# The order of VectorE's work within a slot of a cross-attention kernel: sums and reciprocal ahead of outputs, remainders and the subtraction of maxima

## The reference, cut to what matters

```python
# x: (128, 128, 320); ctx: (128, 128, 512); 20 heads of 16 channels
SEGS = [(0, 77), (77, 81), (81, 85), (85, 128)]
q = heads(x @ to_q_w)
out = 0
for (a, e), wk, wv in zip(SEGS, key_weights, value_weights):    # 512 x 320 each
    k, v = heads(ctx[:, a:e] @ wk), heads(ctx[:, a:e] @ wv)
    p = softmax(q @ k.T / sqrt(16))                             # over this segment alone
    out += p @ v
return merge(out) @ to_out_w + to_out_b + x
```

## Time and profile before

| | |
|---|---|
| median of 3 runs | 1812.3 us (1810.25 to 1822.74) |
| the profiled execution's own time | 1827.61 us |
| its span, first to last instruction | 1825.8 us |
| mean granted PE clock | 0.979 |
| busy: PE, PE weight loads, DVE, ACT, POOL | 93%, 76%, 82%, 57%, 68% |
| instructions | 48271 |

### The profile page before, as it was taken

The page is one execution under the profiler, slowest core; times in us unless marked ns, Lnnn a source line. Parts: engine busy times, 40 slices in busy tenths (PEclk is TensorE's granted clock), DMA queues, the critical chain, the costliest instruction groups (busy, mean ns, idle before and its releaser), DMA issues.

```text
span 1825.8 us, 48271 instructions
## 1 busy us (share of the span) xinstructions
PE 1690.6 (93%) x15120; PEld 1383.0 (76%) x15120; DVE 1495.5 (82%) x3536; ACT 1040.9 (57%) x1860; POOL 1249.3 (68%) x1452
## 2 busy tenths in 40 slices
PE   6859999999999999999999999999999999999987
PEld 3547777788777778777777877777787777787765
DVE  4148988988888888888898888889888888888897
ACT  1135666665565566565666656566665655665564
POOL 3237677767766766777776777677677767767644
PEclk9979999999999999999999999999999999999999
DMA  7678987887888787888788788878878887877861
GB/s 281 171 201 194 222 199 208 214 205 211 206 212 198 204 208 198 200 213 205 211 216 201 210 205 219 209 203 215 208 205 200 210 201 202 209 197 180 211 125 37
DMA packets 409172, 366.24 MB, mean 201 GB/s; under 512 B 17137, under 2 KB 380210, under 8 KB 404786
## 3 DMA queue, kind: packets, MB, share of 16 engines
q1 hardware_dynamic: 409138, 365.79, 79.5%
HBM read 216.30 MB, written 149.42 MB: 200 GB/s over the span
## 4 chain that ended last, share of the span: by engine, by line
PE 67%; DVE 17%; issue 8%; ACT 4%; DMA 1%; DVEq 0%; SPq 0%; ACTq 0%; POOL 0%; POOLq 0%
PE job_ps L786 28%; PE ring_ps L852 10%; PE ring_ps L872 8%; PE ring_ps L865 7%; DVE l_seg L667 6%; PE s_ps L825 4%; PE job_ps L802 4%; DVE probs L640 4%; DVE rest L657 2%; DVE m_seg L624 2%; PE ring_ps L753 2%; ACT probs L543 2%; PE job_ps L796 1%; PE job_ps L805 1%; ACT parts L525 1%
## 5 line engine op out<-in xcount | busy, mean ns | idle before, releaser
L463 POOL TENSOR_TENSOR probs<-probs,rl 128x616 f32<-128x616 f32 (+1 forms) x640 | 628.8, 1005 | 362.6 <-DVE rl L678 357.6
L786 PE MATMUL job_ps<-c_in,w_kv 128*128 128x172 f32 (+1 forms) x2560 | 576.9, 368 | 22.0 <-DVE rest L657 22.0
L552 ACT ACTIVATE pT<-ring_ps 128x512 f32<-128x512 f32 x640 | 378.3, 598 | 356.8 <-PE ring_ps L852 348.2
L786 PEld LDWEIGHTS job_ps<-c_in,w_kv 128*128 128x128 f32 x2560 | 424.5, 190 | 111.2 <-DVE rest L657 29.7
L667 DVE TENSOR_REDUCE l_seg<-probs 128x8 f32<-128x616 f32 (+1 forms) x640 | 385.8, 645 | 56.3 <-ACT probs L543 56.3
L852 PE MATMUL ring_ps<-ident,probs 128*128 128x128 f32 x2560 | 389.4, 277 | 9.3 <-DVE y L687 8.0
L640 DVE TENSOR_TENSOR probs<-s_ps,m_seg 128x616 f32<-128x616 f32 (+1 forms) x640 | 387.3, 647 | 0.0
L624 DVE TENSOR_REDUCE m_seg<-s_ps 128x8 f32<-128x616 f32 (+1 forms) x640 | 368.9, 618 | 0.0
L543 ACT ACTIVATE probs<-probs 128x1024 f32<-128x1024 f32 x320 | 337.5, 1055 | 15.8 <-DVE probs L644 15.8
L852 PEld LDWEIGHTS ring_ps<-ident,probs 128*128 128x128 f32 x2560 | 290.4, 143 | 64.5 <-issue 25.4
L657 DVE TENSOR_TENSOR rest<-job_ps,parts 128x512 f32<-128x512 f32 (+1 forms) x192 | 130.7, 681 | 144.6 <-ACT parts L525 144.6
(11 more groups left out here) (47 smaller groups left out, 1402.9 us busy)
## 6 DMA issues: line engine op xcount, KB each, us to landing
q_all<-q_scratch SPq DMA_DIRECT2D x64, 960.0 KB, 8.5
k_all<-k_scratch SPq DMA_DIRECT2D x64, 960.0 KB, 12.7
c_in<-in_cT SPq DMA_DIRECT2D x32, 1024.0 KB, 5.0
x_raw<-in_xT SPq DMA_DIRECT2D x32, 768.0 KB, 4.4
q_scratch<-parts SPq DMA_DIRECT2D x64, 384.0 KB, 3.0
k_scratch<-parts SPq DMA_DIRECT2D x64, 384.0 KB, 2.5
x_res<-in_x SPq DMA_DIRECT2D x128, 160.0 KB, 3.4
out<-y SPq DMA_DIRECT2D x128, 160.0 KB, 2.9
```

Of the source, the lines that this page charges most:

```text
L463: pool.tensor_tensor(pr[:, :, a:e], pr[:, :, a:e], r[:, :, s:s + 1].broadcast_to((P, OH, e - a)), ALU.mult)
L552: act.activation(pT[:, h:h + QH, :], ring_ps[i][:, :].rearrange("p (h s) -> p h s", h=QH), ACT.Copy)\
L786: last = pe.matmul(dst[:, :, a:e], w_kv[:, l, k, i * P:(i + 1) * P], c_in[:, k, :, a:e], start=(k == 0), stop=(k == CK - 1))
```

## The change

In a slot DVE now takes the maxima of octet n+1, then at once the sums and the reciprocal of octet n, then the outputs, the remainders of both kinds, and last the subtraction of the maxima of octet n+1. Before, the order was: maxima of n+1, outputs, remainders of jobs that ended at 0, subtraction of maxima of n+1, sums of n, remainders of jobs that ended at 1, reciprocal of n. All instructions stay as they are, and the other engines are not touched.

```diff
                 if live(gg, G):
                     reduce_max(gg, o)
+                if live(g, G):
+                    sum_up(g, n)
+                    invert(g, n)
                 for at, (nn, kind, what) in enumerate(FILLS):
                     if nn == (n - 1) % NO and kind == "y" and live(g * NB + what, B):
                         add_residual(g + what // NB, what % NB, at % 2)
-                for turn, job in ended(g, n - 1, 0):
-                    if job in SPLITS:
-                        subtract_part(turn, job)
+                for at in range(2):
+                    for turn, job in ended(g, n - 1, at):
+                        if job in SPLITS:
+                            subtract_part(turn, job)
                 if live(gg, G):
                     shift(gg, o)
-                if live(g, G):
-                    sum_up(g, n)
-                for turn, job in ended(g, n - 1, 1):
-                    if job in SPLITS:
-                        subtract_part(turn, job)
-                if live(g, G):
-                    invert(g, n)
```

## The result

| | before | after |
|---|---|---|
| median of the runs | 1816.97 us (1810.25 to 1822.74, 4 runs) | 2037.52 us (2035.76 to 2038.18, 4 runs) |
| profiled execution | 1827.61 us | 2036.92 us |
| mean granted PE clock | 0.979 | 0.950 |

What follows compares the result with a forecast made beforehand. PE was taken to set the pace, waiting on DVE's releases. 1808.7 us without clock falls, plus 145.5 for gates in 30 groups and 5 for the last groups, made 1959; with 71 for the clock, 2030 us, range 1945 to 2085.

Steps and rivals of the forecast that it cites:

- slot 2: The first transposes wait for the output of slot 1's projection: PE 0.73 us later in each group.
- slots 3 and 4: The late subtraction for octet 4 delays slot 4's sums, output and q0's remainder: q1's products start 2.75 us later.
- slot 5: q2's products wait for q1's remainder, which moves ahead of the subtraction of maxima: the 1.72 us wait goes.
- slot 8: kv1's first half waits for kv0's remainder, now behind exponential, sums and reciprocal: PE 3.09 us later.
- The chain through ACT: Each moved release gets PE, ACT copies, exponential, sums and reciprocal in front of it; gates sum to 4.85 us a group.
- The clock: Behind PE's waits in slots 8 and 4, 45 of 60 bring falls to 1.2 GHz, 1.58 us each: 71 us.
- The ends: In the last two groups, two output gates each, 1 to 1.5 us apiece: 5 us added.
- (a): Rival: PE's gates come as worked out in all groups but the clock stays up: 1959 us, chance 0.2.
- (b): Rival: the exponential is exposed in every slot, 10 us a group more than before: 2112 us, chance 0.1.
- (c): Rival: slot 8 costs 3.1 us but slots 2 to 4 nothing, 1.4 us a group: 1855 us, chance 0.05.
- (d): Rival: not slower; second-kind remainders precede the subtraction, q2's 1.72 us wait and its clock falls go: 1757 us, chance 0.04.
- The other two signs: Prediction wrong if slot 8's exponential starts before kv0's copy, or if the period stays under 55 us.

Runs made afterwards that it cites:

- the kernel with the filled wait: The changed kernel with 32 unused transposes on PE in slot 8, just before kv1's products wait for kv0's remainder: 1969.7 us.
- q1's alone: The kernel before, with q1's remainder in slot 5 taken right behind the maxima instead of behind the sums: 1792.8 us, 0.982 of the kernel before.
- q1's and q2's: The kernel before, with q1's remainder (slot 5) and q2's (slot 6) taken right behind the maxima: 1749.8 us, 0.9646 of the kernel before.

## Why the prediction was right

**What bounds it.** PE sets the pace and DVE matters by when it releases PE: shown. With kv0's release alone put back, the other waits stayed the same to 0.01 us.

**The gates.** The no-fall period was put at 57.9 us; it is 57.66 (the kernel with the filled wait). Its starts, to be held against 881.26, 889.92, 896.97 and 910.78:

```profile
1004.45 0.66 PE L849 MATMUL ring_ps<-ident,probs 128*128 128x128 f32 x4 [0.73 <-DVE y L687]
...
1015.80 0.50 PE L799 MATMUL job_ps<-x_hi,w_q 128*128 128x512 f32 x1
...
1020.91 0.49 PE L799 MATMUL job_ps<-x_hi,w_q 128*128 128x512 f32 x1
...
1037.77 2.34 PE L783 MATMUL job_ps<-c_in,w_kv 128*128 128x308 f32 x8 [0.23 <-DVE rest L657]
```

Term by term, from start to start: slot 2 at +0.73, measured +0.81 (24.34 from kv1's start at 980.11, against 23.53 from the one at 857.73, a period of 53.05 ahead of 910.78); slots 3 and 4 at +2.75, measured +2.69 (11.35 against 8.66); slot 5 at -1.72, measured -1.94 (5.11 against 7.05); slot 8 at +3.09, measured +3.05 (16.86 against 13.81). So the worst sized was slot 5: I took the idle time that the row of q2's products shows, and their start gained 0.2 us more than that. The sum is 57.66 - 53.05 = 4.61 us and not 4.85, 138 us in 30 groups and not 145.5.

**The chain through ACT.** Shown twice: the exponential 1.0 us earlier took 1.0 us off the wait, and outputs or remainders in front of the sums took the slot 8 and slot 2 waits away.

**The clock.** The step was 45 falls of 1.58 us, 71 us. The mean period is 60.35 us, so the clock costs 60.35 - 57.66 = 2.69 us a group, 81 us. In the 30 groups the falls are 30 at slot 8 and 21 behind slot 4, 51 rather than 45, at 1.6 us each. The count was a guess between bounds, and its closeness is partly luck: the experiments show that the same wait of 2.17 us brings a fall in 21 of 30 groups (changed kernel), in 10 (filled wait) or in one (kv0's remainder back). The Trainium skill ("TensorE: Matmul & The Clock Gate", "HAM oscillation") tells of a matmul kernel whose wait for data in each round is long enough that PE starts every round at the lower clock. In the changed kernel slot 8's wait of 3.72 us did so in every group, slot 4's of 2.17 us in two groups of three.

**The ends.** 2036.9 - 1808.7 - 138 - 81 = 9 us, against 5. Some 1.6 us of it stand in group 0: the first kv1 products of slot 8 start 4.6 us later than before (164.74 against 160.10), and 3.04 of that is the gate. There PE waits 1.35, 1.34 and 0.34 us for the subtraction, a place at which I had counted nothing. The rest, some 7 us, stands behind the last of the 30 gates of slot 8. How it divides there between waits and clock was not worked out.

**The rivals.** (a), the clock stays up, falls by the window at 0.50. (b), exposure in every slot, had DVE's idle time right and its price wrong: DVE waits 392.9 us for exponentials where it waited 56.3, 11 us a group more, but this is idle time of an engine that has it to spare. The period without falls is 57.66 us and not 63. (c) falls with the waits of 0.73 and 2.17 us in slots 2 and 4. (d) falls for the whole change, but its useful part was real: without the rest it gives 3.5%.

**The signs.** Of the three signs of being wrong, one was set wrongly. It asked whether kv0's remainder starts less than 2 us after the exponential's end. It starts 1.67 us after (1309.52 to 1311.19), so by the sign the chain would be refuted. But the prediction's own working had 1.66 there (911.46 to 913.12), and the experiments show the chain. The other two signs did not come.

## What to carry to other kernels

When an engine's order is changed, don't add up its work; list what it releases (a bank, a buffer) and, for each release, the chain that now stands ahead of it, and compare that with when the waiting engine wants it. An operation that waits for a long chain belongs behind the short releases that others need, even if, as here, this engine is idle a quarter of the time. A release may be moved ahead of work by itself, and the gate behind it has to be looked at in the same step: q1's alone gave 1.8%, q1's and q2's 3.5%.

## What the runs showed of the hardware that was not expected

A short wait of PE may cost again through the clock, and its length alone doesn't say how often: 2.17 us of wait in slot 4 brought PE to 1.2 GHz in 21, 10 or 1 of 30 groups of three kernels, whose other waits and periods differ. What decides it was not shown. Nor is the price of a fall fixed: 1.1 to 2.6 us with the remainders in front of the sums, 1.2 to 1.6 with the filled wait. That is why moving one remainder was worth 171 us where its wait was worth 91. And PE given 3.66 us of useless transposes in place of a 3.72 us wait made the kernel 67 us faster, though every real instruction stayed in its place in the order.
